# The third step of r's block solution moves from VectorE to GpSimd for ten of sixteen batches

## The chip, the cores and the metric

The kernel runs on one core of a Trainium2 chip. The core has five engines that work at the same time, each with its own queue of instructions: TensorE (PE), VectorE (DVE), ScalarE (ACT), GpSimd (POOL) and SyncE (SP), which here issues nearly all DMA transfers. Engines meet at semaphores: one instruction raises a semaphore when it ends, another waits until it has reached a count. An engine runs its queue in order, so whatever stands behind a waiting instruction waits too.

The metric is the device time of one execution in microseconds (us), the median of several executions.

## The reference

The model has two layers on an input of 16 batches, 512 tokens, 128 features. Only the first layer's attention matters for the change. With a normed input `xn`, it computes

```
static_out = xn @ W.T
k = rmsnorm(xn per head of 8 features)          # q = k
S = lam * S                                      # one 8x8 state per head and batch
err = v_t - k_t S          with v = -static_out
S = S + beta * outer(k_t, err)
o_t = k_t S
out = layernorm(static_out + o)
```

for 16 heads, token after token. The rest of the first layer is a gated network with four hidden matrices of ternary weights, and the second layer is a linear attention with a causal decay mask and a low-rank feed-forward part.

## The kernel before

The token recurrence is regrouped into blocks of four tokens (`BLK = 4`). Within a block, what the four tokens do to one another is a small triangular system. The function `prepare` solves it ahead of the recurrence, for all blocks of a batch at once, and stores the results; `recur_and_second_layer` then runs the recurrence over blocks, with all the rest beside it. `prepare` takes about the first 145 us of the execution.

`prepare` handles one batch (128 features by 512 tokens) at a time, in a software pipeline over loop index k = 0 to 18: each engine writes out, for each k, the stages of several batches, k being the newest. For batch n the stages around the change are:

1. ACT `static` (L512) copies `xnT @ W` from PSUM into `rr[n % 2]`, the right-hand side of r. It first waits (`reuse`, semaphore `st_r`) until the two stores of batch n-2 from the same buffer have landed.
2. DVE `products` (L647) makes the products of keys of different places of a block; PE `couplings` (L779) sums them over the heads' features into the PSUM tile `in_ps`; ACT `couplings` (L522) copies them into `coup[n % 2]` in SBUF and raises `coup_ok`.
3. The triangular system has three steps, j = 0, 1, 2. Each is one call of `sweep` (L265 and L269): a multiplication of the couplings by the solved place j, and an addition into the places after j. Step 0 handles 384 elements of each partition, step 1 256, step 2 128. DVE does it for r (in `rr`, couplings read from PSUM, semaphore `r_step`), POOL does it for P (in `pp`, couplings read from SBUF, semaphore `p_step`). Both semaphores count six per batch, and `sweep` waits in front of every instruction for the count just below its own.
4. SP `store_r` (L329, L301) waits until `r_step` has counted all six of batch n, and issues two transfers from `rr`: `first_r` and `scratch_R`. `store_p` does the same for P.
5. ten of the batches have beside them a group of 512 hidden weight columns: PE transposes it (`weights`, L799), ACT rounds it (`upper`, L534), DVE takes the remainder (`lower`, L664).

The orders of the engines that matter, in terms of one batch n, read: ACT after `couplings(n)`: root, `keys(n+1)` (L507), `normed(n+2)` (L499), `static(n+1)` (L512), `root_mean` (L494), `factors(n)` (L529), `norm(n+3)` (L483), `upper` (L534), `square` (L490), `key_squares(n+1)` (L516), `couplings(n+1)`. PE before `couplings(n+1)` (L779): `factors(n)` (L789), `weights` (L799), which waits for ACT `factors(n)`, and `static(n+2)` (L771). POOL after `coup_ok` of batch n: `solve(n, 0)`, `outgoing(n+1)` (L403), `solve(n, 1)`, `scaled(n+1)` (L395, which waits for the stores of `pp` of batch n-1), `solve(n, 2)`.

Of the kernel before, what the change touches and what calls it, by code (L numbers as in the profile page):

```python
# [14 lines left out]
P = 128  # L15
# [8 lines left out]
BSEG = SEG // BLK  # L24
# [94 lines left out]
def at(s, stage, *more):  # L119

    if s is not None:
        stage(s, *more)


def prepare(nc, io, scr, c):
# [9 lines left out]
    NSEG = L // SEG  # L135
    PLACES = [P, BLK - 1, NSEG, (BLK - 1) * BSEG]
    SWEEPS = 2 * (BLK - 1)
    PEAKS = 4
    POWERS_AT = 2
    with ctx:  # L140
        def sb(name, shape, dt=F32):
            return ctx.enter_context(nc.sbuf_tensor("p_" + name, shape, dt))

        def sem(name):
            return ctx.enter_context(nc.semaphore("p_" + name))
# [7 lines left out]
        def pb(name):  # L153
            return ctx.enter_context(nc.psum_tensor("p_" + name, [P, NT, P], F32))
# [17 lines left out]
        coup = two("coup", PLACES)  # L172
        rr = two("rr", [P, L])
        tmp_p = sb("tmp_p", [P, BLK - 1, NSEG, BSEG])
        ps_x, ps_k, ps_s, ps_f = pb("ps_x"), pb("ps_k"), pb("ps_s"), pb("ps_f")
        ps_n = ctx.enter_context(nc.psum_tensor("p_ps_n", [P, BLK - 1, L], F32))
        ps_t = ctx.enter_context(nc.psum_tensor("p_ps_t", [P, L], F32))
# [15 lines left out]
        r_step, p_step = sem("r_step"), sem("p_step")  # L193
# [29 lines left out]
        groups += [[nath[:, w, o, i * P:(i + 1) * P] for o in range(NB)] for w in range(2) for i in range(NB)]  # L223
        groups += [[nat3[:, i * P:(i + 1) * P] for i in range(NB)]]
        NG = len(groups)

        MATS_AT = {g - 1: g for g in range(2, NG)}

# [42 lines left out]
        def arrived(g):  # L271

            if g < 2:
                return mat_in[g], 16
            if g == NG - 1:
                return mat_in[4], 16
            return mat_in[2 + g % 2], 16 * (g // 2)

        def of(n):

            return Sequence(None, n) if 0 <= n < B else None
# [9 lines left out]
        with nc.allow_non_contiguous_dma(reason='a few hundred words of scales and per-head factors'), nc.Block() as block:  # L291
            @block.sync
            def _(sp):
# [9 lines left out]
                def load_weights(g):  # L303
                    if 2 + 2 <= g < NG - 1:
                        sp.wait_ge(*arrived(g - 2))
# [80 lines left out]
            def _(pool):  # L386
# [20 lines left out]
                def solve(n, j):  # L407
# [2 lines left out]
                        pool.wait_ge(p_in, n.count(1, 3))  # L410
                    sweep(pool, n, pp[n.slot][:, :], coup[n.slot], tmp_p, p_step, j)

                pool.memset(c.ident[:, :], 0.0).then_inc(pool_chain, 1)
                pool.memset(c.head_ones[:, :], 1.0).then_inc(pool_chain, 1)
                pool.memset(c.tri[:, :], 1.0).then_inc(pool_chain, 1)
# [50 lines left out]
                for k in range(1, B + 3):  # L466
                    at(of(k - 2), scaled)
                    at(of(k - 3), solve, 2)
                    at(of(k - 2), solve, 0)
                    at(of(k - 1), outgoing)  # L470
                    at(of(k - 2), solve, 1)

            @block.scalar
            def _(act):
# [42 lines left out]

                def couplings(n):
                    act.wait_ge(p_step, n.count(SWEEPS, SWEEPS))
                    act.wait_ge(n_mm, n.count(1, 2))  # L520
                    for d in range(1, BLK):
                        ins = act.activation(coup[n.slot][:, d - 1, :, earlier(d)], in_ps[:, d - 1, :, earlier(d)], ACT.Copy)  # L522
                    ins.then_inc(coup_ok, 1)
# [75 lines left out]
            def _(dve):  # L599
# [126 lines left out]
                for k in range(B + 3):  # L726
                    at(of(k), statistics)
                    at(of(k), aggregate)
                    if 0 <= k - 3 < NG - 1:
                        lower(k - 3)  # L730
                    elif k - 3 == NG - 1:
                        last_weight()
                    at(of(k - 1), square_sums)
                    at(of(k - 3), solve, 0)
                    at(of(k), scale)
                    at(of(k), offset)
                    at(of(k - 3), solve, 1)
                    at(of(k - 2), products)
                    at(of(k - 3), solve, 2)
                    at(of(k - 1), inverse_rms)  # L740
                    at(of(k - 1), keys)
                    if k == 1:
                        added_row()
                        decays()
                    largest(k)
                    if k == POWERS_AT:
                        powers()
                whether_lower()

            @block.tensor  # L750
            def _(pe):
                def normed(m):
                    pe.wait_ge(xn_ok, m.count(1, 1))
                    pe.wait_ge(xT_ok, m.count(1, 1))
                    for t in range(NT):
                        ins = nc.tensor.transpose(ps_x[:, t, :], xn[m.slot][:, t, :], c.ident[:, :])
                    ins.then_inc(x_tr, 1)

                def keys(m):
                    pe.wait_ge(keys_ok, m.count(1, 1))  # L760
                    pe.wait_ge(kT_ok, m.count(1, 1))
                    pe.wait_ge(prod_ok, m.count(1, 2))
                    for t in range(NT):
                        ins = nc.tensor.matmul(ps_k[:, t, :], keys_t[:, t, :], c.by_place[:, :], start=True, stop=True)
                    ins.then_inc(k_tr, 1)

                def static(m):
                    pe.wait_ge(xT_ok, m.count(1, 2))
                    pe.wait_ge(r_in, m.count(1, 1))
                    pe.wait_ge(ws_ok, 1)  # L770
                    nc.tensor.matmul(ps_s[:, :, :].rearrange("p a b -> p (a b)"), c.ws_t[:, :],  # L771
                                     xnT[m.slot][:, :].rearrange("p (s b i) -> p s i b", i=BLK, b=BSEG), start=True, stop=True).then_inc(s_mm, 1)

                def couplings(n):
                    pe.wait_ge(prod_ok, n.count(1, 3))
                    pe.wait_ge(coup_ok, n.count(1, 1))
                    pe.wait_ge(r_step, n.count(SWEEPS, 2 * SWEEPS))
                    for d in range(1, BLK):
                        ins = nc.tensor.matmul(in_ps[:, d - 1, :, earlier(d)], c.head_ones[:, :], prod[:, d - 1, :, earlier(d)],  # L779
                                               start=True, stop=True)  # L780
                    ins.then_inc(n_mm, 1)

                def factors(n):
                    pe.wait_ge(k2_ok, n.count(1, 1))
                    pe.wait_ge(lo_done, min(n.off + 1, NG - 1))
                    if n.off >= NG - 1:
                        pe.wait_ge(w3_done, 1)
                    pe.wait_ge(fac_ok, n.count(1, 1))
                    nc.tensor.matmul(ps_f[:, :, :].rearrange("p a b -> p (a b)"), c.head_ones[:, :], k2[:, :],  # L789
                                     start=True, stop=True).then_inc(f_mm, 1)  # L790

                pe.sem_inc(x_tr, 2)
                pe.sem_inc(k_tr, 1)
                pe.sem_inc(n_mm, 1)
                def weights(g):
                    pe.wait_ge(*arrived(g))
                    reuse(pe, fac_ok, g + 1 if g > 0 else 0)
                    for n, square in enumerate(groups[g]):
                        ins = nc.tensor.transpose(ps_f[:, n, :], square, c.ident[:, :])  # L799
                    ins.then_inc(tr_done, 1)  # L800

                def unread_products(n):

                    for _ in range(n):
                        nc.tensor.matmul(ps_n[:, 0, 0:P], c.head_ones[:, :], c.ident[:, :], start=True, stop=True)

                pe.wait_ge(const_done, 4)
                pe.wait_ge(ws_in, 16)
                nc.tensor.transpose(ps_s[:, 0, :], nat_ws[:, :], c.ident[:, :]).then_inc(ws_tr, 1)
                for k in range(1, B + 3):  # L810
                    if k == 2:
                        unread_products(12)
                    at(of(k - 2), static)
                    if k < B + 2:
                        at(of(k - 3), couplings)
                    at(of(k - 2), keys)
                    at(of(k - 1), normed)
                    at(of(k - 3), factors)
                    if k == B + 1:
                        couplings(of(B - 1))  # L820
                    if 0 <= k - 2 < NG:
                        weights(k - 2)
                pe.wait_ge(powers_ok, 1)
                pe.wait_ge(r_in, B + 1)
                for n in range(NT):
                    ins = nc.tensor.transpose(ps_s[:, n, :], dec_t[:, n * P:(n + 1) * P], c.ident[:, :])
                ins.then_inc(dec_tr, 1)
                for n in range(PEAKS):
                    pe.wait_ge(peak_done, n + 1)
                    ins = nc.tensor.transpose(ps_x[0:1, n, :], peak[:, n:n + 1], c.ident[:, :])  # L830
                ins.then_inc(peak_tr, 1)
# [1913 lines left out]
```

## Time and profile before

| | |
|---|---|
| median of 3 executions | 786.87 us (785.19 to 788.82) |
| the profiled execution | 788.71 us |
| its span from the first to the last instruction | 787.0 us |
| granted TensorE clock, mean | 0.978 of full |
| busy over the span | PE 720.8, DVE 730.8, POOL 645.2, ACT 587.0 us |

The profile is of one execution. A row of the time line gives the start, the duration, the engine, the line, the operation, the result and its inputs, the shape, and a count when neighbours of one line are merged; in brackets stands how long the engine had been idle before it and what ended that. Times are from the start of the span.

### The profile page before, as it was taken

The numbers are of one execution on the slowest core, as the hardware profiler recorded it, in microseconds if no ns is written. First come the engines' busy times: TensorE is split into PE (matmuls) and PEld (weight loads), VectorE is DVE, ScalarE is ACT, GpSimd is POOL, SyncE is SP. The second block draws the span as 40 slices with busy tenths as digits, with TensorE's granted clock in tenths as the row PEclk, the third lists the DMA queues.
The fourth block names the chain that finished last, engine by engine and source line by source line (L and its number), as shares of the span: only waits on it lengthen the run. The fifth ranks groups of instructions, "written<-read, shape, count | busy, mean of one in ns | idle before, by whom it ended". The sixth has DMA issues, their size and how long they took to land.

```text
span 787.0 us, 13144 instructions
## 1 busy us (share of the span) xinstructions
PE 720.8 (92%) x3365; PEld 524.0 (67%) x3365; DVE 730.8 (93%) x2036; ACT 587.0 (75%) x1363; POOL 645.2 (82%) x640
## 2 busy tenths in 40 slices
PE   5878797599999999999999999887789999999998
PEld 3545453368888888888888888753455666666655
DVE  5999999799999999999999999997799888899887
ACT  7797886779888988898988898775665566657631
POOL 3687789697888998979898799768799789889873
PEclk9899999899999999999999999999999999999999
DMA  5676866500711416162171150511522212121001
GB/s 128 213 248 221 276 223 212 160 15 15 147 40 45 103 42 145 40 129 58 40 146 42 31 116 28 169 41 45 176 78 84 68 37 72 54 67 29 1 27 41
DMA packets 139242, 75.75 MB, mean 96 GB/s; under 512 B 74923, under 2 KB 123053, under 8 KB 139181
## 3 DMA queue, kind: packets, MB, share of 16 engines
q1 hardware_dynamic: 138124, 74.58, 33.8%
q10 hardware_dynamic: 1056, 0.52, 0.2%
q8 instruction: 18, 0.29, 0.2%
q14 instruction: 44, 0.35, 0.2%
HBM read 39.86 MB, written 33.55 MB: 93 GB/s over the span
## 4 chain that ended last, share of the span: by engine, by line
DVE 46%; PE 26%; issue 4%; ACT 2%; POOL 2%; DMA 0%; SPq 0%; DVEq 0%; POOLq 0%; ACTq 0%
DVE r_rec L1271 11%; DVE r_gain L1283 9%; DVE r_pg L1257 9%; DVE r_kw L1277 9%; PE f_ps L2429 7%; PE f_ps L2430 6%; DVE r_rec L1291 6%; PE f_ps L2406 4%; PE r_rec L2458 2%; PE r_rec L2464 1%; DVE l_qs L1345 1%; PE r_rec L2448 1%; PE f_ps L2437 1%; PE f_ps L2397 1%; PE f_ps L2388 1%
## 5 line engine op out<-in xcount | busy, mean ns | idle before, releaser
L1672 POOL TENSOR_TENSOR l_kv<-l_qkv 128x1024 f32<-128x1024 f32 x64 | 124.7, 1952 | 18.5 <-PE f_ps L2430 18.4
L1271 DVE TENSOR_REDUCE r_rec<-r_pg 128x32 f32<-128x288 f32 x256 | 119.5, 467 | 0.6 <-ACT r_pg L1891 0.6
L1283 DVE TENSOR_REDUCE r_gain<-r_kw 128x64 f32<-128x256 f32 x256 | 108.8, 425 | 0.0
L2293 PE MATMUL f_ps<-f_gh,w_hi 128*128 128x512 f32 x256 | 100.0, 391 | 1.1 <-POOL f_gl L1542 1.0
L1542 POOL TENSOR_TENSOR f_hl<-f_h,f_hh 128x512 fp32r<-128x512 f32 x64 | 80.9, 1297 | 24.5 <-ACT f_hh L1937 24.2
L2293 PE MATMUL f_ps<-f_hh,w_hi 128*128 128x512 f32 x256 | 99.8, 390 | 0.0
L1345 DVE TENSOR_TENSOR l_qs<-f_ps,l_qd 128x1024 f32<-128x1024 f32 x64 | 78.1, 1221 | 22.5 <-PE f_ps L2430 16.2
L1550 POOL TENSOR_TENSOR f_g<-f_a,f_b 128x512 f32<-128x512 f32 x64 | 82.4, 1297 | 16.7 <-ACT f_b L1926 16.7
L1542 POOL TENSOR_TENSOR f_gl<-f_g,f_gh 128x512 fp32r<-128x512 f32 x64 | 82.7, 1304 | 0.0
L1352 DVE TENSOR_REDUCE l_o_in<-l_qs 128x128 f32<-128x1024 f32 x64 | 77.2, 1211 | 0.5
L1291 DVE SCALAR_TENSOR_TENSOR r_rec<-r_rec,lam,r_gain 128x64 f32<-128x64 f32 x256 | 76.5, 299 | 0.0
L2429 PE MATMUL f_ps<-l_kv,tri 128*128 128x512 f32 x128 | 68.2, 615 | 7.4 <-DVE l_qs L1345 6.5
L2295 PE MATMUL f_ps<-f_hl,w_hi 128*128 128x512 f32 x192 | 74.7, 389 | 0.0
L2295 PE MATMUL f_ps<-f_gl,w_hi 128*128 128x512 f32 x192 | 74.7, 389 | 0.0
L2076 ACT ACTIVATE l_qkv<-f_ps 128x384 f32<-128x384 f32 x64 | 31.3, 489 | 50.4 <-PE f_ps L2406 49.9
L2430 PE MATMUL f_ps<-l_kv,tri 128*128 128x512 f32 x128 | 65.8, 595 | 0.0
L1932 ACT ACTIVATE f_gh<-f_g 128x512 fp32r<-128x512 f32 x64 | 41.0, 640 | 28.9 <-POOL f_g L1550 28.9
L2329 PEld LDWEIGHTS f_ps<-w,f_e 128*128 128x128 f32 x512 | 60.7, 195 | 1.3
L2329 PE MATMUL f_ps<-w,f_e 128*128 128x128 f32 x512 | 60.7, 277 | 0.0
L2293 PEld LDWEIGHTS f_ps<-f_gh,w_hi 128*128 128x128 f32 x256 | 48.1, 188 | 12.3 <-POOL f_gl L1542 2.6
L1257 DVE TENSOR_TENSOR r_pg<-r_rec,r_pt 128x256 f32<-128x256 f32 x128 | 55.5, 433 | 0.0
L1277 DVE TENSOR_TENSOR r_kw<-r_rec,r_kb 128x256 f32<-128x256 f32 x128 | 55.4, 433 | 0.0
(229 smaller groups left out, 2117.2 us busy)
## 6 DMA issues: line engine op xcount, KB each, us to landing
scratch_xnT<-p_xnT SPq DMA_DIRECT2D x16, 256.0 KB, 2.4
scratch_K<-p_kout SPq DMA_DIRECT2D x16, 256.0 KB, 2.3
scratch_fac<-p_fac SPq DMA_DIRECT2D x16, 256.0 KB, 2.0
scratch_R<-p_rr SPq DMA_DIRECT2D x16, 256.0 KB, 2.4
scratch_P<-p_pp SPq DMA_DIRECT2D x16, 256.0 KB, 3.1
first_x<-scratch_xnT SPq DMA_DIRECT2D x16, 256.0 KB, 3.5
first_xt<-in_L_attn_x_dram SPq DMA_DIRECT2D x16, 256.0 KB, 3.0
scratch_W<-r_w SPq DMA_DIRECT2D x16, 256.0 KB, 4.2
```

The lines of the kernel that those rows point to most:

```text
L1257: dve.tensor_tensor(pg[q][:, at, :, :, 0:DH].rearrange("p (v g) i k -> p v g i k", g=G)[:, :, g, :, :], of_group(g, state[q]).rearrange("p ...
L1271: dve.tensor_reduce(w_here(g, blk), pg[q][:, at, :, :, :].rearrange("p (v g) i k -> p v g i k", g=G)[:, :, g, :, :], AX.X, ALU.add).then_i ...
L1277: dve.tensor_tensor(of_group(g, kw).rearrange("p (v k) i -> p v k i", k=DH), w_here(g, blk).unsqueeze(2).to_broadcast([P, DH, DH, BLK]), b ...
L1283: dve.tensor_reduce(of_group(g, gain), of_group(g, kw), AX.X, ALU.add).then_inc(gain_ok, 1)
L1291: dve.scalar_tensor_tensor(out=of_group(g, state[after]), in0=of_group(g, state[q]), scalar=c.lam4[:, :], in1=of_group(g, gain), op0=ALU.m ...
L1542: pool.tensor_tensor(lower, full, upper.bitcast(F32), ALU.subtract).then_inc(done, 1)
L1672: pool.tensor_tensor(dst, k, v, ALU.mult).then_inc(kv_ok, 1)
L2293: nc.tensor.matmul(bank, c.w_hi[:, weights[k], :], upper[k], start=k == 0, stop=False)
L2295: nc.tensor.matmul(bank, c.w_hi[:, weights[k], :], lower[k], start=False, stop=False)
L2329: ins = nc.tensor.matmul(y[:, tokens], e_f[:, k, tokens], c.w3[:, k, :], start=False, stop=t == NT - 1 and k == NB - 1)
L2429: nc.tensor.matmul(to[:, 0, :], c.tri[:, :], kv[s % 2][:, 0, :], start=True, stop=True)
L2430: nc.tensor.matmul(to[:, 1, :], c.tri[:, :], kv[s % 2][:, 1, :], start=True, stop=True).then_inc(tri_mm, 1)
```

## The change

For batches 0 to 9, the third step of r's solution (`sweep` with j = 2, 128 elements) leaves DVE's queue. POOL gets it, with the couplings from `coup` in SBUF and a buffer of its own, as the last thing of each loop index k. Batches 10 to 15 keep the step on DVE. PE's `couplings` waits for two counts of `r_step` less where the third step of the batch before is no reader of PSUM, and ACT's `couplings` gets a wait on `r_step` before it overwrites `coup`. `NG` is 11, so `ON_GPSIMD` is 10.

```diff
+        tmp_last = sb("tmp_last", [P, 1, NSEG, BSEG])
...
+        ON_GPSIMD = NG - 1
...
+                def solve_r_last(n):
+                    pool.wait_ge(r_step, n.count(SWEEPS, 2 * SWEEPS + 4))
+                    sweep(pool, n, rr[n.slot][:, :], coup[n.slot], tmp_last, r_step, 2)
...
                     at(of(k - 2), solve, 0)
                     at(of(k - 1), outgoing)
                     at(of(k - 2), solve, 1)
+                    if k - 3 < ON_GPSIMD:
+                        at(of(k - 3), solve_r_last)
...
                 def couplings(n):
                     act.wait_ge(p_step, n.count(SWEEPS, SWEEPS))
+                    act.wait_ge(r_step, n.count(SWEEPS, SWEEPS))
...
-                    at(of(k - 3), solve, 2)
+                    if k - 3 >= ON_GPSIMD:
+                        at(of(k - 3), solve, 2)
...
-                    pe.wait_ge(r_step, n.count(SWEEPS, 2 * SWEEPS))
+                    pe.wait_ge(r_step, n.count(SWEEPS, 2 * SWEEPS - (2 if 1 <= n.off <= ON_GPSIMD else 0)))
```

Below is POOL's queue in the steady part of the preparation, from one `solve(n, 0)` to the next. The rows into `p_tmp_p` and `p_pp` with 384, 256 and 128 elements are the three steps for P, `p_kout` is `outgoing`, and `p_pp<-p_kT,pfac` is `scaled`. Before:

```order
L265 TENSOR_TENSOR p_tmp_p<-p_coup,p_pp 128x384 [waits p_p_step,p_p_in,p_coup_ok]
L269 TENSOR_TENSOR p_pp<-p_pp,p_tmp_p 128x3x8x16 [waits p_p_step]
L403 TENSOR_TENSOR p_kout<-p_kT,kfac 128x512 [waits p_st_k1,p_factors_ok,p_kT_ok]
L265 TENSOR_TENSOR p_tmp_p<-p_coup,p_pp 128x256 [waits p_p_step]
L269 TENSOR_TENSOR p_pp<-p_pp,p_tmp_p 128x2x8x16 [waits p_p_step]
L395 TENSOR_TENSOR p_pp<-p_kT,pfac 128x512 [waits p_factors_ok,p_out,p_small_in,p_kT_ok]
L265 TENSOR_TENSOR p_tmp_p<-p_coup,p_pp 128x128 [waits p_p_step]
L269 TENSOR_TENSOR p_pp<-p_pp,p_tmp_p 128x8x16 [waits p_p_step]
```

The same place of POOL's queue after the change (lines of the changed kernel, three to ten higher):

```order
L268 TENSOR_TENSOR p_tmp_p<-p_coup,p_pp 128x384 [waits p_p_step,p_p_in,p_coup_ok]
L272 TENSOR_TENSOR p_pp<-p_pp,p_tmp_p 128x3x8x16 [waits p_p_step]
L406 TENSOR_TENSOR p_kout<-p_kT,kfac 128x512 [waits p_st_k1,p_factors_ok,p_kT_ok]
L268 TENSOR_TENSOR p_tmp_p<-p_coup,p_pp 128x256 [waits p_p_step]
L272 TENSOR_TENSOR p_pp<-p_pp,p_tmp_p 128x2x8x16 [waits p_p_step]
L268 TENSOR_TENSOR p_tmp_last<-p_coup,p_rr 128x128 [waits p_r_step]
L272 TENSOR_TENSOR p_rr<-p_rr,p_tmp_last 128x8x16 [waits p_r_step]
L398 TENSOR_TENSOR p_pp<-p_kT,pfac 128x512 [waits p_factors_ok,p_out,p_small_in,p_kT_ok]
L268 TENSOR_TENSOR p_tmp_p<-p_coup,p_pp 128x128 [waits p_p_step]
L272 TENSOR_TENSOR p_pp<-p_pp,p_tmp_p 128x8x16 [waits p_p_step]
```

Where the first row belongs to batch n, the two new rows belong to batch n-1: they stand behind the first two steps for P of batch n.

On DVE, the stretch from the second step of r for batch n to the first step for batch n+1 reads as follows before (`p_prod` is `products`, `p_ps_t` the PSUM buffer of the sweeps):

```order
L269 TENSOR_TENSOR p_rr<-p_rr,p_ps_t 128x2x8x16 [waits p_r_step]
L647 SCALAR_TENSOR_TENSOR p_prod<-p_ps_k,cfac,p_kT 128x384 [waits p_factors_ok,p_kT_ok,p_n_mm]
L647 SCALAR_TENSOR_TENSOR p_prod<-p_ps_k,cfac,p_kT 128x8x32
L647 SCALAR_TENSOR_TENSOR p_prod<-p_ps_k,cfac,p_kT 128x8x16
L265 TENSOR_TENSOR p_ps_t<-p_ps_n,p_rr 128x128 [waits p_r_step]
L269 TENSOR_TENSOR p_rr<-p_rr,p_ps_t 128x8x16 [waits p_r_step]
L631 RECIPROCAL p_ps_t<-p_rms 128x64 [waits p_rms_ok]
...
L265 TENSOR_TENSOR p_ps_t<-p_ps_n,p_rr 128x384 [waits p_r_step,p_r_in,p_coup_ok]
```

And after:

```order
L272 TENSOR_TENSOR p_rr<-p_rr,p_ps_t 128x2x8x16 [waits p_r_step]
L657 SCALAR_TENSOR_TENSOR p_prod<-p_ps_k,cfac,p_kT 128x384 [waits p_factors_ok,p_kT_ok,p_n_mm]
L657 SCALAR_TENSOR_TENSOR p_prod<-p_ps_k,cfac,p_kT 128x8x32
L657 SCALAR_TENSOR_TENSOR p_prod<-p_ps_k,cfac,p_kT 128x8x16
L641 RECIPROCAL p_ps_t<-p_rms 128x64 [waits p_rms_ok]
...
L268 TENSOR_TENSOR p_ps_t<-p_ps_n,p_rr 128x384 [waits p_r_step,p_r_in,p_coup_ok]
```

Two instructions of the third step are gone from DVE's queue; the first step still waits on `p_r_step`, now raised by POOL's pair.

## Rows read from the trace of the kernel before

**Rows 1.** Busy time by engine over ten batches of the preparation
```profile
31.30:110.80 79.50, 64.58 (x253) 37.45 (x252) 73.06 (x240) 64.80 (x159) 62.91 (x80) 0.92 0.74 246
```

**Rows 2.** Waits in 30 to 111 us, DVE's and ACT's longest
```profile
DVE p_ps_t L265 <- ACT p_coup L522: 2.5, 4, 0.8
ACT p_coup L522 <- PE p_ps_n L779: 15.7, 11, 2.2
```

**Rows 3.** Time line of ACT: couplings of four batches, and static between
```profile
30.32 0.94 ACT L522 ACTIVATE p_coup<-p_ps_n 128x384 f32<-128x384 f32 x3 [1.60 <-PE p_ps_n L779]
...
70.56 0.94 ACT L522 ACTIVATE p_coup<-p_ps_n 128x384 f32<-128x384 f32 x3 [0.92 <-PE p_ps_n L779]
...
72.61 0.61 ACT L512 ACTIVATE p_rr<-p_ps_s 128x512 f32<-128x512 f32 x1
...
78.01 0.94 ACT L522 ACTIVATE p_coup<-p_ps_n 128x384 f32<-128x384 f32 x3 [0.92 <-PE p_ps_n L779]
...
109.84 0.94 ACT L522 ACTIVATE p_coup<-p_ps_n 128x384 f32<-128x384 f32 x3 [1.72 <-PE p_ps_n L779]
```

**Rows 4.** Time line of DVE in the batch that starts at 71.5 us
```profile
71.53 0.57 DVE L265 TENSOR_TENSOR p_ps_t<-p_ps_n,p_rr 128x384 f32<-128x384 f32 x1
...
73.75 1.26 DVE L647 SCALAR_TENSOR_TENSOR p_prod<-p_ps_k,cfac,p_kT 128x384 f32<-128x384 f32 x3
...
75.25 0.29 DVE L269 TENSOR_TENSOR p_rr<-p_rr,p_ps_t 128x128 f32<-128x128 f32 x1
```

**Rows 5.** Time line of POOL in the same batch
```profile
71.57 1.00 POOL L265 TENSOR_TENSOR p_tmp_p<-p_coup,p_pp 128x384 f32<-128x384 f32 x1 [1.19 <-ACT p_coup L522]
...
75.41 0.73 POOL L269 TENSOR_TENSOR p_pp<-p_pp,p_tmp_p 128x256 f32<-128x256 f32 x1
...
77.10 0.46 POOL L265 TENSOR_TENSOR p_tmp_p<-p_coup,p_pp 128x128 f32<-128x128 f32 x1
77.63 0.45 POOL L269 TENSOR_TENSOR p_pp<-p_pp,p_tmp_p 128x128 f32<-128x128 f32 x1
```

**Rows 6.** Time line of DVE and SP around the first stores of r
```profile
27.74 0.29 DVE L269 TENSOR_TENSOR p_rr<-p_rr,p_ps_t 128x128 f32<-128x128 f32 x1
...
28.05 0.55 SPq L329 DMA_DIRECT2D first_r<-p_rr  x1
28.65 0.59 SPq L301 DMA_DIRECT2D scratch_R<-p_rr  x1
```

**Rows 7.** DMA issues: count, size, median us from issue to landing
```profile
scratch_R<-p_rr SPq DMA_DIRECT2D x16, 256.0 KB, 2.4
scratch_P<-p_pp SPq DMA_DIRECT2D x16, 256.0 KB, 3.1
```

**Rows 8.** Time line of PE: slow and fast runs of weights, static, couplings
```profile
25.78 1.09 PE L799 MATMUL p_ps_f<-ident,p_nat 128*128 128x128 f32 x4 [1.06 <-ACT p_fac L529]
26.66 1.99 PE L771 MATMUL p_ps_s<-p_xnT,ws_t 128*128 128x512 f32 x2
...
60.02 2.74 PE L779 MATMUL p_ps_n<-p_prod,head_ones 128*128 128x384 f32 x6
...
74.18 0.63 PE L799 MATMUL p_ps_f<-ident,p_nath 128*128 128x128 f32 x4 [1.53 <-ACT p_fac L529]
74.65 1.96 PE L771 MATMUL p_ps_s<-p_xnT,ws_t 128*128 128x512 f32 x2
76.43 1.48 PE L779 MATMUL p_ps_n<-p_prod,head_ones 128*128 128x384 f32 x6
...
135.08 2.90 PE L779 MATMUL p_ps_n<-p_prod,head_ones 128*128 128x384 f32 x6 [3.24 <-DVE p_rr L269]
...
147.01 2.07 PE L2353 MATMUL f_ps<-w_hi 128*128 128x512 f32 x4 [3.52 <-issue]
```

**Rows 9.** PE busy (count), granted clock, DMA share, GB/s in two stretches
```profile
138.00:139.00 1.00, 1.00 (x3) 0.85 0.06 23
...
151.00:152.00 1.00, 1.00 (x4) 0.52 0.96 200
```

## The prediction

> **What bounds the kernel now.** I read the stretches of the preparation first, then the waits in it, then the time lines of the four engines over one batch. From the end of ACT's couplings of batch 1 (31.26) to that of batch 11 (110.78) ten batches take 79.5 us, 7.95 each [rows 3], and DVE is busy for 73.1 of them, more than any other engine [rows 1]. So DVE looks like the bound. The waits qualify this: DVE waits for ACT's couplings four times, 2.5 us in all, and ACT waits for PE's couplings eleven times, 15.7 us in all [rows 2]. Two loops are nearly equal: DVE's own queue, and a loop through ACT and PE. The second is to be seen in one batch: ACT's couplings end at 71.50, `static` starts at 72.61, the next couplings end at 78.95 [rows 3], a period of 7.45 us.
>
> I write T for the end of ACT's couplings of batch n, which lets both DVE and POOL begin step 0 of batch n: they start at 71.53 and 71.57, with T = 71.50 [rows 4, 5].
>
> **What is removed.** The last pair on DVE: products end at 73.75 + 1.26 = 75.01, the pair ends at 75.25 + 0.29 = 75.54, so 0.53 us a batch [rows 4], 5.3 us over ten batches. It is worth that only where DVE's queue is what ends the batch. The buffer `tmp_last` costs nothing, as it is only memory. PE's shorter count lets it pass 0.5 us sooner after the products; it waits for the products anyway.
>
> **What is added, and where it stands.** The pair on POOL is 77.63 + 0.45 - 77.10 = 0.98 us [rows 5]. POOL is busy for only 62.9 of 79.5 us [rows 1], so there is room for it. But it stands in a bad place. `sweep` waits for the full count of `r_step`, so DVE's step 0 of batch n now needs POOL's pair of batch n-1; and in POOL's queue that pair stands behind `solve(n, 0)`, `outgoing(n+1)` and `solve(n, 1)`, which themselves start only at T. Before, DVE had finished batch n-1 by itself long before T. Step by step:
>
> - POOL's five instructions of batch n end at 75.41 + 0.73 = 76.14, that is T + 4.64 [rows 5]. The pair ends at T + 5.6.
> - DVE begins step 0 at T + 5.65 in place of T + 0.03. Queued behind it are the rest of the sweeps, `offset` (for which ACT's `norm` waits) and `products`. The products ended 75.01 - 71.53 = 3.5 us after step 0 began [rows 4], so now at T + 9.15.
> - SP's `store_r` of batch n-1 waits for the same count. Its first transfer was issued 0.02 us after the count was reached (27.74 + 0.29 = 28.03 to 28.05), `scratch_R` 0.60 later [rows 6], and that lands after 2.4 us [rows 7]: T + 5.6 + 0.02 + 0.60 + 2.4 = T + 8.65.
> - ACT's `static` of batch n+1 writes the same buffer `rr` and waits for these two landings. Before, they had landed in time and `static` started at T + 1.11 [rows 3]. Now it starts at T + 8.7.
> - From the start of `static` to the end of the next couplings is 78.95 - 72.61 = 6.34 us [rows 3]. Nothing in it can be skipped: `factors` lets PE do `weights`, behind which stand `static` and `couplings` in PE's queue (74.18, 74.65, 76.43 [rows 8]), and ACT copies the result at 78.01. So the next T is T + 15.05.
>
> What else ends in the loop is hidden under it: DVE's products at T + 9.15 are done before PE's couplings, which start 76.43 - 72.61 = 3.8 us after `static`, at T + 12.5. SP issues `load`, the weights and `first_p` between `scratch_R` and the store of P, four issues of about 0.6 us [rows 6], so P starts at about T + 8.6 and lands at T + 11.7 [rows 7]; `scaled`, about 1 us, and P's last pair are done by T + 13.7. That leaves 1.3 us before POOL is late for the next T.
>
> **TensorE's clock.** PE now idles for about 9 us of each period. Of two pauses of 3.24 and 3.52 us before work at 135.08 and 147.01 [rows 8], both were followed by work at half clock, 1.2 of 2.4 GHz: it was full again some 3.3 us after the first restart (0.85 in 138 to 139) and 5 us after the second (0.52 in 151 to 152) [rows 9]. At half clock, `weights` takes 1.09 in place of 0.63, `static` 1.99 in place of 1.96, `couplings` 2.74 in place of 1.48 [rows 8]: 1.75 us more, all of it on the path. Couplings start 2.7 us after PE restarts, so with the clock back after 3.3 us only 0.3 of their 1.26 is lost, 0.8 us in all; with 5 us, all of it. The bounds are 0 and 1.75 us; I take 1.25, the middle of the two restarts. The period is 16.3 us.
>
> The Trainium skill, "TensorE: Matmul & The Clock Gate", section "HAM oscillation — how this bites in real kernels", says that a loop with a long enough pause in every turn starts every turn at half clock. The rows before show it in some batches only (the couplings at 60.02 at 2.74, those at 76.43 at 1.48 us [rows 8]), with much shorter pauses. With the page's rule the period would be up to 16.8, with a fall in three batches of ten as before about 15.5.
>
> The Trainium skill, "GPSIMD Engine Reference", section "4.1 Engine selection", advises against elementwise work of two inputs on GpSimd, being about twice as slow. The rows say 0.98 against 0.53 us, a factor of 1.8; the duration alone would not hurt here.
>
> **The sum.** Ten periods lengthen: those from batch 1 to batch 11, since DVE's steps of batches 1 to 10 wait for POOL's pairs of 0 to 9. 10 x 16.3 = 163 us against 79.5: 83.5 us more. Batches 11 to 15 and the recurrence run as before, only later; the recurrence needs the last batch's results, so nothing takes the delay back. The profiled execution took 788.71 (span 787.0) and would take 872.2; on the median of 786.87 that is 870.4 us.
>
> **The rivals.**
>
> 1. The store does not gate, only DVE's new wait does. For it: no row shows ACT waiting for the stores of r. Against it: those landed in time only because r was complete at 75.54. The period would be T + 9.15 for the products, then PE's couplings 1.48, and ACT's 0.94 with two hand-overs of 0.1: 11.7 us, or 12.9 at half clock. Ten are 117 to 129, so 37.5 to 49.5 more: 824 to 836 us. Chance 0.10.
> 2. The other side: POOL's pair is done before DVE asks for it. Then DVE's queue is 0.53 us shorter in the batches in which it ends the period, about seven of ten (in the others PE is slow, as at 60.02); 3.7 us at most, 783 us. It decides if the pair ends before T + 0.03, which needs it ahead of `solve(n, 0)` in POOL's queue, where it doesn't stand. Chance 0.03, and 0.02 for no change.
> 3. It is worse: the slack of 1.3 us before POOL is late is used up, because the stores land later than their medians, or PE stays slow for keys too. With 2 us more a period: 890 us. Chance 0.10.
> 4. The change does what it says but the periods are not all hit, for example the first and the last: two fewer are 17 us less, 854 us. Chance 0.07.
>
> **How the numbers follow.** My forecast has 0.68. Its own range is 857 (no clock loss, 15.05 a period) to 876 (all at half clock, 16.8). The range for 8 in 10 reaches down to the half-clock end of the first rival and up towards the third: 835 to 884 us. About 0.5% is what a measurement can tell from no change. Faster: 0.03. Within 0.5%: 0.02. Slower: 0.95.
>
> **What would show it.** In the new profile: DVE waits for POOL's `p_rr` before step 0, about 5.6 us each, ten times; ACT's `static` waits for the DMA `scratch_R` (or `first_r`) about 7 us each, ten times; `p_coup` comes every 15 to 17 us for ten batches and every 7 us then; the granted clock in this stretch falls from 0.92 to about 0.7. A wait of DVE on POOL without one of ACT on the DMA is rival 1. No wait of DVE on POOL would prove the whole reasoning wrong.

## The result and the profile after

| | before | after |
|---|---|---|
| median of the runs taken together | 785.86 us (785.09 to 788.82, 5 runs) | 868.54 us (868.22 to 871.93, 5 runs) |
| ratio | | 1.1039 (95% interval 1.1012 to 1.1067) |
| span of the profiled execution | 787.0 us | 866.5 us |
| granted clock, mean | 0.978 | 0.939 |

The change makes the kernel 10.4% slower; the forecast was 870.4 us, range 835 to 884. The ratios with their intervals, here and below, are not quotients of the two medians, and leave out two executions far off all others (one of 4051 us of a kernel below, one of 1051 us of the kernel before). The page of the changed kernel shows where the time goes: busy times, and the rows of TensorE, its granted clock and DVE over 40 slices of 21.7 us.

```profile
PE 726.1 (84%) x3365; PEld 530.2 (61%) x3365; DVE 727.7 (84%) x2016; ACT 588.9 (68%) x1363; POOL 654.3 (76%) x660
...
PE   5553453457699999999999999998778999999998
...
DVE  6734533549899999999999999999879888999887
...
PEclk9877667679799999999999999999999999999999
```

The work is nearly that of before: DVE has 3 us less, POOL 9 us more (twenty instructions). DVE's slices from the second to the ninth are at 3 to 7 tenths, and the clock is at 6 to 8 tenths in the same slices. The same stretch as in [rows 1], from the couplings of batch 1 to those of batch 11, in the view by stretches:

```profile
30.50:191.80 161.30, 73.16 (x258) 46.44 (x257) 70.60 (x223) 66.08 (x160) 71.63 (x100) 0.71 0.37 121
```

161.3 us in place of 79.5, with DVE busy for 70.6 where it was 73.1, and a clock of 0.71 in place of 0.92. The waits in 20 to 240 us, whose counterparts are [rows 2] (total, number, longest):

```profile
DVE p_ps_t L268 <- POOL p_rr L272: 83.1, 10, 9.0
DVE p_ps_t L268 <- ACT p_coup L532: 2.6, 3, 1.5
...
ACT p_rr L521 <- DMA scratch_R<-p_rr: 73.0, 11, 7.6
ACT p_coup L532 <- PE p_ps_n L790: 28.3, 14, 3.0
...
POOL p_pp L398 <- DMA scratch_P<-p_pp: 64.1, 11, 7.1
```

Three engines wait for ten batches, for three different things. Which one counts cannot be read off the totals: the longest, DVE's 83.1 us, is nearly the whole loss, and the experiments show that it alone is not it. The time line of one period, over all engines, answers to [rows 3 to 6] and [rows 8]:

```profile
100.35 0.46 POOL L268 TENSOR_TENSOR p_tmp_last<-p_coup,p_rr 128x128 f32<-128x128 f32 x1
100.89 0.45 POOL L272 TENSOR_TENSOR p_rr<-p_rr,p_tmp_last 128x128 f32<-128x128 f32 x1
101.37 0.55 SPq L332 DMA_DIRECT2D first_r<-p_rr  x1
101.47 0.57 DVE L268 TENSOR_TENSOR p_ps_t<-p_ps_n,p_rr 128x384 f32<-128x384 f32 x1 [8.91 <-POOL p_rr L272]
...
101.96 0.59 SPq L304 DMA_DIRECT2D scratch_R<-p_rr  x1
...
103.69 1.26 DVE L657 SCALAR_TENSOR_TENSOR p_prod<-p_ps_k,cfac,p_kT 128x384 f32<-128x384 f32 x3
...
104.32 0.60 ACT L521 ACTIVATE p_rr<-p_ps_s 128x512 f32<-128x512 f32 x1 [7.30 <-DMA scratch_R<-p_rr]
...
105.88 1.09 PE L810 MATMUL p_ps_f<-ident,p_nath 128*128 128x128 f32 x4 [8.97 <-DMA p_nath<-in_L_ffn_h_w_dram]
...
106.76 1.99 PE L782 MATMUL p_ps_s<-p_xnT,ws_t 128*128 128x512 f32 x2
...
107.47 1.04 POOL L398 TENSOR_TENSOR p_pp<-p_kT,pfac 128x512 f32<-128x512 f32 x1 [6.13 <-DMA scratch_P<-p_pp]
...
108.56 2.74 PE L790 MATMUL p_ps_n<-p_prod,head_ones 128*128 128x384 f32 x6
```

The couplings before it ended at T = 95.77. POOL's pair ends at 101.34, T + 5.57; DVE starts at T + 5.70; the store of r lands and ACT's `static` starts at T + 8.55; DVE's products are done at T + 9.18, long before PE takes them at T + 12.79, at half clock. PE's first row puts its wait down to the load of a weight, but the load that SP issues in this period is for a later group; the group that PE transposes here was loaded two periods before (issued at 69.97). `weights` follows ACT's `factors`, which ended at 105.73. For nine other waits at this place the profile names `factors` itself. Three periods, as the couplings of ACT show them:

```profile
94.83 0.94 ACT L532 ACTIVATE p_coup<-p_ps_n 128x384 f32<-128x384 f32 x3 [2.55 <-PE p_ps_n L790]
...
111.42 0.94 ACT L532 ACTIVATE p_coup<-p_ps_n 128x384 f32<-128x384 f32 x3 [2.64 <-PE p_ps_n L790]
...
128.04 0.94 ACT L532 ACTIVATE p_coup<-p_ps_n 128x384 f32<-128x384 f32 x3 [2.64 <-PE p_ps_n L790]
...
143.60 0.94 ACT L532 ACTIVATE p_coup<-p_ps_n 128x384 f32<-128x384 f32 x3 [1.60 <-PE p_ps_n L790]
```

### The profile page after: what moved, and what is told of

Same layout as the page of the kernel before. It is cut to its first block, busy times and chain, and to the rows that moved or that the text cites. A ratio compares the mean times of both kernels' runs of the same rounds, so it can differ in the third digit from the quotient of the medians.

```text
span 866.5 us, 13154 instructions
## 1 busy us (share of the span) xinstructions
PE 726.1 (84%) x3365; PEld 530.2 (61%) x3365; DVE 727.7 (84%) x2016; ACT 588.9 (68%) x1363; POOL 654.3 (76%) x660
## 4 chain that ended last, share of the span: by engine, by line
PE 45%; DVE 18%; POOL 3%; issue 3%; ACT 3%; DMA 1%; SPq 0%; DVEq 0%; ACTq 0%; POOLq 0%
PE f_ps L2304 9%; PE f_ps L2440 6%; PE f_ps L2441 6%; PE f_ps L2306 5%; DVE r_rec L1282 4%; PE f_ps L2417 4%; DVE r_pg L1268 3%; PE f_ps L2311 3%; DVE r_gain L1294 3%; DVE r_kw L1288 3%; PE f_ps L2340 3%; DVE r_rec L1302 2%; PE r_rec L2475 1%; PE r_rec L2469 1%; PE r_rec L2459 1%
## 5 line engine op out<-in xcount | busy, mean ns | idle before, releaser
L1683 POOL TENSOR_TENSOR l_kv<-l_qkv 128x1024 f32<-128x1024 f32 x64 | 124.8, 1953 | 16.3 <-PE f_ps L2441 16.2
L1282 DVE TENSOR_REDUCE r_rec<-r_pg 128x32 f32<-128x288 f32 x256 | 116.1, 453 | 0.6 <-ACT r_pg L1902 0.6
L1294 DVE TENSOR_REDUCE r_gain<-r_kw 128x64 f32<-128x256 f32 x256 | 105.4, 412 | 0.0
L1356 DVE TENSOR_TENSOR l_qs<-f_ps,l_qd 128x1024 f32<-128x1024 f32 x64 | 78.2, 1221 | 20.8 <-PE f_ps L2441 14.9
L268 DVE TENSOR_TENSOR p_ps_t<-p_ps_n,p_rr 128x384 f32<-128x384 f32 (+2 forms) x38 | 17.6, 464 | 85.9 <-POOL p_rr L272 83.1
L1302 DVE SCALAR_TENSOR_TENSOR r_rec<-r_rec,lam,r_gain 128x64 f32<-128x64 f32 x256 | 73.1, 286 | 0.0
L810 PE MATMUL p_ps_f<-ident,p_nath 128*128 128x128 f32 x32 | 8.7, 427 | 71.1 <-ACT p_fac L539 62.1
L398 POOL TENSOR_TENSOR p_pp<-p_kT,pfac 128x512 f32<-128x512 f32 x16 | 16.6, 1041 | 64.1 <-DMA scratch_P<-p_pp 64.1
```

The costliest lines, as they stand in the source:

```text
L1282: dve.tensor_reduce(w_here(g, blk), pg[q][:, at, :, :, :].rearrange("p (v g) i k -> p v g i k", g=G)[:, :, g, :, :], AX.X, ALU.add).then_i ...
L1294: dve.tensor_reduce(of_group(g, gain), of_group(g, kw), AX.X, ALU.add).then_inc(gain_ok, 1)
L1302: dve.scalar_tensor_tensor(out=of_group(g, state[after]), in0=of_group(g, state[q]), scalar=c.lam4[:, :], in1=of_group(g, gain), op0=ALU.m ...
L1356: dve.tensor_tensor(qs[s % 2][:, :].rearrange("p (h v k) -> p h v k", h=H, k=DH), score_banks(s)[:, :, :].rearrange("p a (h v k) -> p (a h ...
L1683: pool.tensor_tensor(dst, k, v, ALU.mult).then_inc(kv_ok, 1)
```

## The experiments

All start from the changed kernel. Times are medians, beside the kernel before on the same chip.

**A semaphore of its own for POOL's pair** takes DVE's wait away and leaves the store's. `r_at` gives the count of `r_step` at which batch n starts: DVE counts four per batch where it does two steps. POOL's pair counts on `last_r`, which SP's store and the reuse of `coup` wait for. A one-shot count (`powers_ok`) moved to another semaphore to make room.

```diff
+        def r_at(n, more):
+            return 2 * SWEEPS + (SWEEPS - 2) * min(n.off, ON_GPSIMD) + SWEEPS * max(n.off - ON_GPSIMD, 0) + more
...
+                    pool.wait_ge(r_step, r_at(n, 4))
+                    sweep(pool, n, rr[n.slot][:, :], coup[n.slot], tmp_last, last_r, 2, 2 * n.off + 1)
...
-                    sweep(dve, n, rr[n.slot][:, :], in_ps, tmp_r, r_step, j)
+                    sweep(dve, n, rr[n.slot][:, :], in_ps, tmp_r, r_step, j, r_at(n, 2 * j))
```

> The changed kernel, in which POOL's pair counts on a semaphore of its own, so that DVE's first step of the next batch does not wait for it; two buffers for r as before. My theory: DVE's 83 us of waits for POOL vanish, but the store of r still lands 8.6 us after the couplings and ACT's static waits for it, so nothing is gained: 868 us (864 to 871). Rival: DVE's wait for POOL is the cause, as the length of its waits in the trace suggests (83.1 us, nearly the whole loss): 787 us.

Measured: 870.66 us against 786.90, ratio 1.1073 (1.1039 to 1.1107); the changed kernel has 1.1039 (1.1012 to 1.1067). Its waits of DVE and of ACT:

```profile
DVE p_ps_t L651 <- ACT p_rms L512: 58.5, 10, 5.9
DVE p_ps_t L273 <- ACT p_coup L542: 31.0, 13, 3.3
...
ACT p_rr L530 <- DMA scratch_R<-p_rr: 74.1, 12, 7.3
```

DVE no longer waits for POOL at all, and idles as long for ACT, 89.5 us in two places. The wait that the trace put first was worth nothing while the other gate stood; ACT's for the store is unchanged, and so is the time.

**Four buffers for r** take the store's gate away and leave DVE's wait. Each buffer has its own semaphore for its stores; a few one-shot counts moved to other semaphores to make room.

```diff
-        rr = two("rr", [P, L])
+        rr = [sb(f"rr{i}", [P, L]) for i in range(4)]
...
-                    reuse(act, st_r[m.slot], both(m))
+                    reuse(act, st_r[m.off % 4], 32 * (m.off // 4))
```

> The changed kernel with four buffers for r in place of two, so that ACT's static no longer waits for the stores of the batch before; DVE's wait for POOL's pair stays. My theory: the store's gate goes and what comes next is POOL: the store of P lands 6.1 us after POOL's pair (the wait of 6.13 before scaled at 107.47), that is 11.7 us after POOL began the batch, and with scaled and the last step for P POOL is ready again after 13.7 us. Ten periods of 13.7 in place of 16.1: 844 us (838 to 850). Rival: only DVE's wait for POOL counts, and the buffers change nothing: 868 us. Rival: after the store only DVE's wait is left, 11.7 to 12.9 us a period: 824 to 836 us.

Measured: 849.99 us against 786.90, ratio 1.0812 (1.0778 to 1.0846), at the upper end of what I expected. POOL in one period:

```profile
88.19 1.00 POOL L267 TENSOR_TENSOR p_tmp_p<-p_coup,p_pp 128x384 f32<-128x384 f32 x1 [0.17 <-POOL p_pp L271]
...
93.24 0.45 POOL L271 TENSOR_TENSOR p_rr<-p_rr,p_tmp_last 128x128 f32<-128x128 f32 x1
...
96.64 0.59 SPq L303 DMA_DIRECT2D scratch_P<-p_pp  x1
...
100.09 1.04 POOL L398 TENSOR_TENSOR p_pp<-p_kT,pfac 128x512 f32<-128x512 f32 x1 [6.40 <-DMA scratch_P<-p_pp]
```

POOL begins the batch the moment its own last step is done (0.17 us idle), so POOL and the store of P, which SP issues behind its wait for the pair, now set the period (13.9 us here).

**The store of P earlier**, alone: SP issues it ahead of the store of r of the same batch.

```diff
-                    at(of(k - 4), store_p)
+                    if k == B:
+                        at(of(k - 4), store_p)
...
                     at(of(k - 2), store_keys)
+                    if k <= B - 2:
+                        at(of(k - 3), store_p)
                     at(of(k - 3), store_r)
```

> The changed kernel, with SP's store of P of a batch issued ahead of the store of r of the same batch, so that it no longer stands behind that wait. My theory: the period of 16.1 us is set by POOL's pair, the store of r and the path through ACT and PE; P is only 2.9 us short of it (POOL's last step for P of one batch ended at 109.46, the next couplings at 112.36). So the 64 us in which POOL waits for the store of P vanish and the time stays at 868 us (865 to 871). Rival: POOL's wait for P holds the loop; then the period falls to about 13 and the time to some 840 us.

Measured: 871.98 us against 786.90, ratio 1.1101 (1.1060 to 1.1142): if anything slower than the changed kernel (1.1012 to 1.1067), with the intervals just overlapping, and 1 us above the range that I expected. POOL's wait for the store of P is gone and turned into one for the couplings:

```profile
POOL p_tmp_p L268 <- ACT p_coup L535: 96.5, 14, 9.7
```

**Both, four buffers and the earlier store of P**, leave DVE's wait alone.

> Four buffers for r and the earlier store of P together. My theory: only DVE's wait for POOL is left, which gives the period of my first rival: 5.65 to DVE's first step, 3.5 to the end of products, 1.5 for PE's couplings, 0.94 for ACT's, 11.7 us at full clock, 12.9 at half: 824 to 836 us. That measures the price of DVE's wait alone: 37 to 50 us over the kernel before. Rival: without the store's gate the kernel is back at 787 us, and DVE's wait is nothing by itself.

Measured: 843.88 us against 786.90 (838.13 to 845.53), ratio 1.0738 (1.0703 to 1.0772). The mechanism was there, 13.25 us a period from 69.88 to 83.14, but more than the 12.9 that I had as its upper end:

```profile
69.88 0.94 ACT L535 ACTIVATE p_coup<-p_ps_n 128x384 f32<-128x384 f32 x3 [1.87 <-PE p_ps_n L793]
...
83.14 0.94 ACT L535 ACTIVATE p_coup<-p_ps_n 128x384 f32<-128x384 f32 x3 [1.86 <-PE p_ps_n L793]
...
89.81 0.57 DVE L267 TENSOR_TENSOR p_ps_t<-p_ps_n,p_rr 128x384 f32<-128x384 f32 x1 [6.05 <-POOL p_rr L271]
...
93.35 2.93 PE L793 MATMUL p_ps_n<-p_prod,head_ones 128*128 128x384 f32 x6 [3.25 <-DVE p_prod L660]
```

From T = 84.08, DVE starts at T + 5.73, PE's couplings 3.54 later, and they take 2.93 us after a pause of 3.25 us: 5.73 + 3.54 + 2.93 + 0.11 + 0.94 = 13.25. I had added 1.2 us for the clock; the couplings alone lose 2.93 - 1.48 = 1.45. So DVE's wait by itself would have cost some 57 us, the clock that falls with it included: it is a second gate, standing behind the store's. The profiled execution, 838.13 us, is the fastest of the six; 13.25 us in place of 12.9 explain it and not the rest of the way to the median.

**Both gates away**: own semaphore, four buffers, earlier store of P.

> Both gates taken away: own semaphore for POOL's pair, four buffers for r, and the earlier store of P. POOL's pair stands where the change put it. My theory: the two gates are all there is, and the time is back at 787 us (783 to 792), perhaps a little above, since POOL has 0.98 us more in each of ten batches. Rival: the work on POOL itself costs, about 1 us a batch: 796 us or more.

Measured: 816.08 us against 787.89, ratio 1.0369 (1.0335 to 1.0402). A miss by 29 us. The time lies where the rival had it (796 or more, for the work on POOL), but not for its reason: further down the same work on POOL costs nothing. Its longest waits in 20 to 190 us:

```profile
DVE p_stats L627 <- DMA p_x<-in_L_attn_x_dram: 33.6, 10, 5.3
...
SPq L340 <- POOL p_rr L277: 42.9, 10, 6.6
```

The input of a later batch is issued by SP behind `store_r`, which still waits for the late pair, so the statistics of that batch wait for x. In the changed kernel the load goes out at T + 6.8 (102.59) and the statistics start without a wait at 106.46: in time for a period of 16 us. Here it goes out at 90.00, T + 7.3 with T = 82.69, and DVE starts the statistics at 93.19, T + 10.5, after idling for 3.13 us: late for a period of 7.5. The next kernel issues x and the weights ahead of `store_r`:

```diff
+                    at(of(k + 2), load)
+                    if k in MATS_AT:
+                        load_weights(MATS_AT[k])
                     at(of(k - 3), store_r)
-                    at(of(k + 2), load)
-                    if k in MATS_AT:
-                        load_weights(MATS_AT[k])
```

> The last kernel (own semaphore, four buffers, earlier store of P) took 816 us, 29 above what I expected, and its trace has DVE waiting 33.6 us in ten batches for the load of x, which SP issues behind its wait for POOL's pair. Here SP issues the load of x and of the weights ahead of the store of r. My theory: that is the third thing held up by the late pair, and the last: 787 us (783 to 792). Rival: DVE's wait for x only hides another bound, POOL's longer queue or ACT's waits for DVE (21.6 us): 800 us or more.

Measured: 795.07 us against 787.99, ratio 1.0074 (1.0048 to 1.0100), 3 us above the range that I expected and under the rival's 800. 21 of the 29 us are back. The rest is still 7 us:

```profile
DVE p_stats L627 <- DMA p_x<-in_L_attn_x_dram: 6.6, 5, 2.2
```

DVE still waits five times for x. SP still issues it behind the store of r of the batch before, and for that store's pair SP waits 24.8 us in all. That these 6.6 us are the rest fits in size, but no run takes them away, so it stays open how much of it is POOL's longer queue.

**POOL's pair in its own batch**: it stands behind `solve(n, 1)` of the same batch n, one loop index earlier, with nothing else changed.

```diff
-                    if k - 3 < ON_GPSIMD:
-                        at(of(k - 3), solve_r_last)
+                    if k - 2 < ON_GPSIMD:
+                        at(of(k - 2), solve_r_last)
```

> The changed kernel with POOL's pair moved by one batch: it stands right behind POOL's second step for P of its own batch, so r is complete 5.6 us after the couplings of its own batch, ahead of the next. My theory: DVE never waits, and the stores land at 8.65 us after the couplings, beside static at 7.45 + 1.1 = 8.55, so ACT waits 0.1 us or not at all: 787 us (782 to 790). DVE's queue is 0.53 us shorter, which can give 2 to 4 us. Rival: the pair on GpSimd costs in itself, wherever it stands: over 800 us.

Measured: 787.68 us against 786.98, ratio 1.0017 (0.9993 to 1.0041). One batch earlier in a queue, and the gates are gone: between 30 and 111 us DVE never waits for POOL or for x, and ACT waits for the store of r twice, 0.8 us in all. With four buffers beside it:

> The same with four buffers for r, so that the stores' landing cannot matter. My theory: the version that gives the change all it can: DVE's queue 0.53 us shorter in the seven of ten batches in which it ends the period, 783 us (780 to 787). Rival: POOL, with 7.3 us of work and its gaps in each batch, is the new bound: 787 to 792 us.

Measured: 787.94 us against 786.98, ratio 1.0001 (0.9979 to 1.0024). So the pair on GpSimd costs nothing by itself, and brings nothing either, within some 2 us both ways. I had expected 783 us. In the first of the two, ten batches take 79.2 us:

```profile
30.70:109.90 79.20, 63.36 (x258) 36.46 (x257) 68.70 (x223) 65.05 (x160) 70.79 (x98) 0.94 0.74 245
```

DVE is busy for 68.7 us in place of 73.1 [rows 1], 4.4 less, and the stretch is 0.3 us shorter. What DVE saves it waits: 6.7 us for ACT's couplings, where it was 2.5 [rows 2].

```profile
DVE p_ps_t L268 <- ACT p_coup L532: 6.7, 6, 2.2
```

DVE's queue did not end these batches. The rival of the second kernel, POOL as the new bound, fits its time, and its trace puts three of ACT's waits before the couplings down to POOL. But in each of them PE's couplings, at half clock, end within 0.1 us of POOL's last step (44.94 + 2.74 = 47.68 against 47.76 in the first), so POOL stands level with PE there, and taking its wait away would give next to nothing.

**Work for TensorE in its pauses**: 34 matmuls of 128 columns, whose results nothing reads, ahead of `weights` in ten batches.

```diff
+                    if 4 <= k <= 13:
+                        pe.wait_ge(xT_ok, k + 1)
+                        for _ in range(34):
+                            nc.tensor.matmul(ps_x[:, 0, :], c.head_ones[:, :], c.ident[:, :], start=True, stop=True)
```

> The changed kernel with 34 matmuls of 128 columns, whose results nothing reads, in PE's queue ahead of weights in ten batches, to fill the 9 us in which PE idles. My theory: the clock stays up or falls more seldom, and the path from static to the next couplings takes 6.3 us as before in place of 8.0: up to 1.7 us less in each of ten periods, 852 to 860 us. Rival: the half clock does not matter for the period, 868 us; or the added matmuls delay weights, above 868 us.

Measured: 857.61 us against 786.98, ratio 1.0897 (1.0862 to 1.0932). The stretch of the ten batches, and the path in one period:

```profile
31.50:182.90 151.40, 140.31 (x938) 112.43 (x937) 69.87 (x221) 65.79 (x160) 71.81 (x100) 0.98 0.39 130
```

```profile
103.31 0.60 ACT L521 ACTIVATE p_rr<-p_ps_s 128x512 f32<-128x512 f32 x1 [7.04 <-DMA scratch_R<-p_rr]
...
108.71 0.94 ACT L532 ACTIVATE p_coup<-p_ps_n 128x384 f32<-128x384 f32 x3 [0.94 <-PE p_ps_n L790]
```

The clock is 0.98 in place of 0.71, and from `static` to the end of the couplings it is 6.34 us again, as in [rows 3]. The period before that row is 14.9 us, where the one before 111.42 in the changed kernel was 16.6. Seven of the ten are of this length, two, in which the clock was low at the couplings, take 16.6 and 16.8 us, and the last 13.6; 11 of the 82 us are back. ACT's wait for the store is as long as before: the clock is an effect of the gates, with a price of its own.

## Why the prediction was right

**The gate of the store.** Forecast: pair at T + 5.6, `static` at T + 8.7. Measured: T + 5.57 and T + 8.55, as `scratch_R` landed after 2.3 us. Four buffers, which take this gate alone away, bring the time from 868.5 to 850.0 us, until the store of P gates; the own semaphore, which leaves it, brings nothing.

**The gate of DVE.** DVE's wait was there ten times, 83.1 us in all. I had written 5.6 us each, counted from T; the trace has 8.3 each, because DVE, with its other work done, was at the wait before T (8.91 us idle until 101.47, so from 92.56). That size was wrong in what to look for, not in the sum, where only the end of the wait counts (T + 5.70 against 5.65).

**The path through ACT and PE.** 6.34 us at full clock was right, shown by the kernel with the filled pauses (109.65 - 103.31).

**The clock.** Forecast 1.25 us a period, between 0 and 1.75. At T = 95.77 the path took 112.36 - 104.32 = 8.04 us, 1.70 more than 6.34; over the nine periods with `weights` it took 6.95 to 8.04 us, 7.73 on average, so 1.39 more. Filling the pauses gave back 11 us over ten periods, 1.1 each, with the clock still low in two of them.

**The sum.** Ten periods of 16.3 against 79.5, 83.5 us more. Measured from the couplings of batch 1 to those of 11: 190.91 - 29.61 = 161.3 us, 81.8 more. Nine of them average 16.3; the tenth is 14.4, with no `weights` in PE's queue, which I had not counted apart. The span grew by 79.5, so 2.3 us came back behind batch 11, where I had said that nothing would; the median grew by 82.7 over the kernel before in the same runs. The mechanism carried the forecast, but that it came within 2 us of the median is in part luck: in the nine periods a `static` 0.11 us early (T + 8.59 on average against 8.7) met a clock 0.14 us dearer, and against the profiled executions, 79.5 apart, the forecast of 83.5 is 4 us too high.

**What was weighed and proved minor.** P was held up as foreseen (7.1 us at most, 64.1 in all) and had slack (POOL's last step for P ended at 109.46, T + 13.7, and the next couplings at 112.36): issued earlier, it gave nothing. The rival without the store's gate is real as a mechanism, but lies under it; its upper end, 836, was 8 us too low, of which 3.5 are the 13.25 in place of 12.9 us a period; the rest no trace shows. The rival on the other side, the pair ahead of DVE's need, is what the pair in its own batch builds: it gives no change, not the 3.7 us at most that I gave it. That price rested on a wrong reading of mine, that DVE's queue ends seven of ten batches. The rows do not bear it: DVE's products are done at 75.01 [rows 4], and PE takes them at 76.43 [rows 8], because `static` stands before them in its queue. The loop through ACT and PE, 7.45 us, was the bound in that batch, and DVE, though busier than any other engine, had 1.4 us to spare at this place.

## What to carry to other kernels

When a step moves to another engine's queue, ask which batch's work stands ahead of it there, and list everybody who waits for its count: here the next step on DVE, a store whose buffer is reused, and all transfers behind that store in one queue. The wait with the largest total in the trace can be worth nothing when another gate ends beside or after it, so take gates away one by one and in pairs. And the engine with the most busy time need not be the bound: look for where its result is waited for. Last, of two positions of an instruction one loop index apart, the one behind the next batch's work cost 82 us, the other none that could be measured.

## What the runs showed of the hardware

Half clock costs the three kinds of matmul on this path differently: couplings 2.74 against 1.48 us, transposes 1.09 against 0.63, but `static`, which reads its 512 columns with a stride, 1.99 against 1.96. `factors`, of the same shape without the stride, takes 1.02 us at full clock (95.88 in the changed kernel) and 2.05 at half (95.26 in the kernel with both gates away). No run varies the stride alone, so that it is the reason is not shown. Where matmuls that nothing reads fill the pauses, the mean granted clock is 0.98; with pauses of 9 us in every period it is 0.71.
